# Shorter register heads, narrower frame copies, and variances ahead of the last sums in small units

## The reference, cut to what matters

```python
def _gn(v, G=32, eps=1e-5):
    g = v.reshape(B_, G, C_ // G, H_, W_)
    m = jnp.mean(g, axis=(2, 3, 4), keepdims=True)
    s = jnp.var(g, axis=(2, 3, 4), keepdims=True)
    return ((g - m) / jnp.sqrt(s + eps)).reshape(v.shape)
# in _displace: offset -> off_int (rounded) and sub (rest); kern = exp(-(kx*kx+ky*ky)/(2*0.5**2)), normalised
shifted = x[:, ch[:, None, None], iyc[:, :, None], ixc[:, None, :]] * mask[None]
out = lax.conv_general_dilated(shifted, kern_c[:, None, :, :], window_strides=(1, 1), padding='SAME', ...)
x = x + _displace(_gn(x), offset)
```

## Time and profile before

| | us |
|---|---|
| median of three runs | 976.3 |
| the profiled execution's own time | 979.06 |
| its span on the core | 977.1 |
| TensorE busy, mean granted clock 0.888 | 785.6 |
| VectorE busy | 824.8 |
| ScalarE busy | 638.9 |
| GpSimd busy | 368.1 |
| data moved | 403.09 MB, 413 GB/s |

### The profile page before, as it was taken

How to read it: one execution, slowest core, us unless ns; L and a number is a source line. 1 busy time by engine, 2 the same in 40 slices (tenths; PEclk the granted TensorE clock), 3 DMA queues, 4 the chain that set the end, 5 groups by cost and what they waited for, 6 DMA issues and landing times.

```text
span 977.1 us, 9088 instructions
## 1 busy us (share of the span) xinstructions
PE 785.6 (80%) x2132; PEld 383.6 (39%) x2132; DVE 824.8 (84%) x551; ACT 638.9 (65%) x461; POOL 368.1 (38%) x348
## 2 busy tenths in 40 slices
PE   0998987979979698897979879689797997979820
PEld 0544443434434343353434434345343443434410
DVE  7587988777798997978889899898998979797795
ACT  7778676564766747678466746577675785774661
POOL 0214034340432624013254393463845438250312
PEclk9999988989979799897998979989898897989955
DMA  9999999999999999999999999999999999999948
GB/s 364 427 401 423 392 405 429 429 429 428 430 429 430 432 428 414 430 429 430 431 429 406 398 433 376 407 419 393 431 408 430 430 427 431 431 431 430 430 208 343
DMA packets 27821, 403.09 MB, mean 413 GB/s; under 512 B 3216, under 2 KB 3216, under 8 KB 3216
## 3 DMA queue, kind: packets, MB, share of 16 engines
q1 hardware_dynamic: 27792, 402.71, 98.0%
HBM read 201.38 MB, written 201.33 MB: 412 GB/s over the span
## 4 chain that ended last, share of the span: by engine, by line
DVE 28%; DMA 27%; PE 20%; POOL 7%; issue 7%; ACT 5%; DVEq 3%; ACTq 2%; SPq 0%; POOLq 0%
PE sum_ps L289 17%; DMA out_dram<-xs 15%; DMA xs<-x_dram 12%; DVE xs L713 6%; DVE xs L716 6%; DVE smooth L709 6%; DVE smooth L704 6%; DVE xs L719 4%; POOL small L253 2%; POOL small L260 2%; ACT frame L417 2%; POOL small L257 2%; ACT unused L484 2%; POOL small L266 1%; ACTq L393 1%
## 5 line engine op out<-in xcount | busy, mean ns | idle before, releaser
L289 PE MATMUL sum_ps<-xs,bands 128*128 128x512 f32 x976 | 483.5, 653 | 51.2 <-DMA xs<-x_dram 51.2
L484 ACT ACTIVATE unused<-xs,small 128x4096 bf16 (+1 forms) x94 | 348.3, 3706 | 8.3 <-ACT small L470 4.8
L417 ACT ACTIVATE frame<-xs,small (+1 forms) x96 | 223.3, 2326 | 184.3 <-DVE smooth L709 183.3
L289 PEld LDWEIGHTS sum_ps<-xs,bands 128*128 128x128 f32 x976 | 200.6, 210 | 295.4 <-issue 282.2
L253 POOL TENSOR_TENSOR small<-small 128x3 f32<-128x3 f32 x32 | 41.6, 1299 | 570.6 <-ACT small L492 570.6
L289 PE MATMUL sum_ps<-xs,halves 128*128 128x512 f32 x496 | 230.0, 619 | 17.4 <-DMA xs<-x_dram 17.4
L704 DVE SCALAR_TENSOR_TENSOR smooth<-frame,side_w 128x612 f32 (+5 forms) x96 | 163.6, 1705 | 72.2 <-ACT frame L417 37.1
L713 DVE SCALAR_TENSOR_TENSOR xs<-smooth,small,xs 128x612 f32 (+5 forms) x96 | 163.5, 1703 | 51.9 <-POOL small L266 49.6
L709 DVE SCALAR_TENSOR_TENSOR smooth<-frame,side_w,smooth x96 | 159.7, 1664 | 7.5 <-DVE smooth L704 4.1
L719 DVE SCALAR_TENSOR_TENSOR xs<-smooth,small,xs 128x594 f32 (+9 forms) x96 | 159.8, 1664 | 3.4
L716 DVE SCALAR_TENSOR_TENSOR xs<-smooth,small,xs 128x594 f32 (+9 forms) x96 | 159.7, 1664 | 3.4
(11 more groups left out here) (132 smaller groups left out, 259.3 us busy)
## 6 DMA issues: line engine op xcount, KB each, us to landing
xs<-x_dram SPq DMA_DIRECT2D x96, 2048.0 KB, 14.8
out_dram<-xs SPq DMA_DIRECT2D x96, 2048.0 KB, 17.7
smooth<-offset_dram SPq DMA_DIRECT2D x1, 48.0 KB, 4.1
```

The source lines that it names most:

```text
L289: last = nc.tensor.matmul(sum_ps[:, :], (FIRST, SAME, SECOND)[i], slot_px(n, c * BANK, (c + 1) * BANK), start=(i == 0 and c == 0), stop=(i ...
L417: nc.scalar.activation(frame[:, bass.ds(b, rows * PITCH)].rearrange("p (r c) -> p r c", c=PITCH)[:, :, LEFT:LEFT + W], xs[:, bass.ds(a, ro ...
L484: nc.scalar.activation(unused[:, :], xs[:, bass.ds(n % SLOTS * PIX, PIX)], ACT.Square, bias=neg_mean[:, i:i + 1], accum_out=squares[:, i:i ...
```

## The change

Four things are changed.

1. **VectorE's head.** The table has a fifth number for each tile (`BESIDE`), so that the head no longer computes the address of the neighbour column. What L709's address needs (`turn`, `behind`) is computed after L704 has been issued. The loop counts from 1, and `side_w` has one more column for it.
2. **ScalarE's copy.** Where the window has 34 columns or fewer, the copy takes 34 columns instead of 64, and 64 or 34 rows: `COPIES` has six sizes (four of 64 columns, then 64x34 and 34x34) instead of four. The table for it is computed by more steps on VectorE at the start.
3. **TensorE's order** in small units: the variances of u stand before the sums of u+1's third tile, as in large ones.
4. **ScalarE's order** in small units: `variances(u)` stands before `sum_means(u + 1)`.

```diff
-    WORDS = 4
-    KIND, TO, FROM, COLUMN = range(WORDS)
+    WORDS = 5
+    KIND, TO, FROM, BESIDE, COLUMN = range(WORDS)
+    NARROW = 2
+    COPIES = [(rows, W) for rows in SIDES] + [(SIDES[k], SIDES[NARROW]) for k in (0, NARROW)]
+    COL_BITS = (W - SIDES[NARROW]).bit_length()
...
-                    early = UT if u % 2 else UT - 1
-                    sums(u + 1, range(early))
+                    sums(u + 1, range(UT - 1))
                     variances(u)
-                    sums(u + 1, range(early, UT))
+                    sums(u + 1, range(UT - 1, UT))
                     means(u + 1)
...
-                row = word & (1 << ROW_BITS) - 1
-                rows_kind = act.snap(word >> ROW_BITS)
+                column = word & (1 << COL_BITS) - 1
+                row = (word >> COL_BITS) & (1 << ROW_BITS) - 1
+                copy_kind = act.snap(word >> ROW_BITS + COL_BITS)
...
-                    rows = SIDES[k]
+                    rows, cols = COPIES[k]
...
-                        frame[:, bass.ds(b, rows * PITCH)].rearrange("p (r c) -> p r c", c=PITCH)[:, :, LEFT:LEFT + W],
-                        xs[:, bass.ds(a, rows * W)].rearrange("p (r c) -> p r c", c=W),
+                        frame[:, bass.ds(b, rows * PITCH)].rearrange("p (r c) -> p r c", c=PITCH)[:, :, LEFT:LEFT + cols],
+                        xs[:, bass.ds(a, rows * W)].rearrange("p (r c) -> p r c", c=W)[:, :, 0:cols],
...
+                variances(u, first)
                 if ahead and not large:
-
                     sum_means(u + 1)
-                variances(u, first)
...
-            chained(V.scalar_tensor_tensor(code[:, :, 0], kind[:, :, 1], float(1 << ROW_BITS), first_row[:, :, 1],
+            chained(V.tensor_scalar(narrow, kind[:, :, 0], float(NARROW), None, ALU.is_ge))
+            chained(V.tensor_scalar(low, kind[:, :, 1], float(NARROW), float(len(SIDES)), ALU.is_ge, ALU.add))
...
+            chained(V.scalar_tensor_tensor(code[:, :, 0], code[:, :, 0], float(1 << COL_BITS), narrow,
                                            ALU.mult, ALU.add))
...
+                turn = kind_of % 2
+                behind = (src + 1 - turn).with_bounds(min_val=1, max_val=most + 1)
...
-                dve.reg_mov(at_turn, kind_of & 1)
-                turn = dve.snap(at_turn, min_val=0, max_val=1)
-                dve.reg_mov(at_behind, src + 1 - turn)
-                dve.reg_mov(at_beside, src + 2 * turn - 1)
-                beside = dve.snap(at_beside, min_val=0, max_val=FRAME_ROWS * PITCH)
+                beside = dve.snap(next_tile[BESIDE], min_val=0, max_val=FRAME_ROWS * PITCH)
```

More of the change, by code:

```diff
@@ L104, in build @@
         base_w = xs[:, SLOTS * PIX:].rearrange("p (n k) -> p n k", k=3)
-        side_w = [sb(f"side_w{k}", [P, TILES]) for k in range(2)]
+        side_w = [sb(f"side_w{k}", [P, TILES + 1]) for k in range(2)]
         words = sb("words", [P, WORDS * (TILES + 1)], i32)
-        fills = sb("fills", [P, TILES], i32)
+        fills = words[HALF:P, 0:TILES]
         setup = smooth[:, 0:11 * 2 * POSITIONS].rearrange("p (n f a) -> p n f a", n=11, a=2)
@@ L404, in fill_frame @@
                 act.reg_mov(frames, u * UT + i)
-                act.reg_mov(copy_from, base + row * W)
-                act.reg_mov(copy_to, row * PITCH + PAD * PITCH)
+                act.reg_mov(copy_from, base + row * W + column)
+                act.reg_mov(copy_to, row * PITCH + column + PAD * PITCH)
+                source = act.snap(copy_from, min_val=0, max_val=SLOTS * PIX)
+                target = act.snap(copy_to, min_val=PAD * PITCH, max_val=FRAME_ROWS * PITCH)
+                done = act.snap(frames, min_val=1, max_val=TILES)
                 if i == 0:
@@ L596, in for_halves @@
                 return column.rearrange("p (j t) -> p j t", t=2 * UT).unsqueeze(2).to_broadcast(
-                    [P, len(PAIRS), HALVES, 2 * UT])
+                    [column.shape[0], len(PAIRS), HALVES, 2 * UT])
             FAR, ROUNDER = 1024.0, 1.5 * 2.0 ** 23
@@ L680, in _, with smooth_tile @@
             V.engine_nop().then_inc(tile_done, 1)
-            next_tile = [dve.alloc_register(name) for name in ("next_kind", "next_to", "next_from", "next_column")]
+            next_tile = [dve.alloc_register(name) for name in
+                         ("next_kind", "next_to", "next_from", "next_beside", "next_column")]
             done_count = dve.alloc_register("done_count")
-            at_turn, at_beside, at_behind = (dve.alloc_register(name) for name in ("turn", "beside", "behind"))
-            def smooth_tile(rows, cols, src, beside, behind, turn, dst, n, done, weights):
+            def smooth_tile(rows, cols, src, beside, kind_of, most, dst, done, weights):
                 under = xs[:, bass.ds(dst, rows * W)]
@@ L700, in smooth_tile @@
                 sm = smooth[:, 0:rows * cols].rearrange("p (r c) -> p r c", c=cols)
-                part = smooth[:, bass.ds(turn, rows * cols)].rearrange("p (r c) -> p r c", c=cols)[:, :, 0:cols - 1]
                 dve.wait_ge(frame_ready, done)
-                V.scalar_tensor_tensor(sm, frame_window(beside, cols), side_w[0][:, bass.ds(n, 1)], frame_window(src, cols),
+                V.scalar_tensor_tensor(sm, frame_window(beside, cols), side_w[0][:, bass.ds(done, 1)], frame_window(src, cols),
                                        ALU.mult, ALU.add
@@ L708, in smooth_tile @@
                 dve.reg_load(next_tile, words[0:1, bass.ds(done * WORDS, WORDS)])
-                V.scalar_tensor_tensor(part, frame_window(behind, cols - 1), side_w[1][:, bass.ds(n, 1)], part,
+                turn = kind_of % 2
+                behind = (src + 1 - turn).with_bounds(min_val=1, max_val=most + 1)
+                part = smooth[:, bass.ds(turn.with_bounds(min_val=0, max_val=1), rows * cols)].rearrange(
+                    "p (r c) -> p r c", c=cols)[:, :, 0:cols - 1]
+                V.scalar_tensor_tensor(part, frame_window(behind, cols - 1), side_w[1][:, bass.ds(done, 1)], part,
                                        ALU.mult, ALU.add
@@ L741, in emit @@
                     smooth_tile(rows, cols, src.with_bounds(min_val=1, max_val=most),
-                                beside.with_bounds(min_val=0, max_val=most + 1),
-                                behind.with_bounds(min_val=1, max_val=most + 1), turn,
+                                beside.with_bounds(min_val=0, max_val=most + 1), kind_of, most,
                                 dst.with_bounds(min_val=0, max_val=(SLOTS - 1) * PIX + (H - rows) * W + W - cols),
-                                n, done, weights)
+                                done, weights)
                 choose(dve, kind_of, 0, len(SIDES) ** 2, emit, 2)
@@ L750, in _ @@
             dve.addr_align(256, max_nops=0)
-            with dve.Fori(0, TILES) as n:
+            with dve.Fori(1, TILES + 1) as n:
                 tile_of(n)
```

50 lines of the change are left out of this document (31 added, 19 removed).

## The result

| | before | after |
|---|---|---|
| median of the runs, us | 976.15 (4 runs, 973.61 to 976.35) | 1017.42 (4 runs, 1012.62 to 1024.46) |
| profiled execution, its own time, us | 979.06 | 1012.62 |
| ratio of the medians | | 1.0435, 95% interval 1.0371 to 1.0498 |

The forecast was 971.9, in a range that ended at 976.5. It was wrong by 45.5 us and in sign. The mechanism that did it was not among the rivals.

The account below looks back on a forecast made before the run. Transfers were taken to bound most of the kernel, VectorE 501 to 747 us and the end. Units 16 to 23 -5.2, new order +0.9, start +0.7, end -0.8 made -4.4: 976.3 to 971.9 us, range 967.5 to 976.5.

Parts of the forecast that it names:

- VectorE's head: Units 16 to 23: 13 exposed heads 0.5 us shorter, 1.0 lost behind the table read, net -5.5 us of VectorE's time.
- The stretch of units 16 to 23, -5.2: 501 to 747 us, VectorE-bound: units 16 to 19 keep 3.4 us, units 20 to 23 can give 1.8.
- if the next part eats it: Low end, -1 us, of the gain in units 16 to 23, should the part after them take it.
- The end, -0.8: From tile 90 on: exposed heads save 1.2 us, L709's longer waits in the last two tiles cost 0.4.
- That the offset is carried over: Whole kernel: the profiled execution's 2.8 us above the median kept, the terms' -4.4 applied to 976.3 us.
- The weights, -2.1: Small units, 501 to 747 us: variances leave earlier, taking 2.1 of L713's 4.2 us wait for weights.
- The new order, +0.9: Small units: the second copy comes 1 to 2.8 us later, costing 0.1 in each of four units, 0.5 later.
- the second copy hands the gain back: Rival, chance 0.20: later sums delay small units' second copy, taking the 3.4 us of units 16 to 19; 975.3 us.
- slower rival: Rival, chance 0.08: in small units TensorE waits for squares before the variances, and its clock may drop; +4.0, 980.3 us.
- the weights come no earlier: Rival, chance 0.10: GpSimd's steps beside VectorE keep L713's 2.1 us wait; +1.0 in units 16 to 19, 972.9 us.
- The start, +0.7: Setup: fourteen more instructions make the first store 1.4 us later; small units 1 and 3 give some back.
- The narrow copies: ScalarE's copies: time goes by elements, 0.86 to 1.6 us shorter each, buying slack only; nothing counted of its own.

Follow-up runs that it names:

- r5s5: The kernel before with the changed kernel's whole table (rows of five words, 20 bytes apart, ScalarE's word in the same tensor): 1027.28 us, ratio 1.0529.
- aligned4: The changed kernel with table rows of four words at multiples of 16 bytes, the weights' column worked out in registers behind L738: 974.36 us, ratio 0.9984.
- r4off8: The kernel before with its table moved by 8 bytes, the read still four words: 1009.26 us, ratio 1.036.
- heads_only: The kernel before with the shorter heads alone, on aligned rows of four words, old order, full-width copies: 974.03 us, ratio 0.998.
- aligned4_order: aligned4 with the old order in small units on both TensorE and ScalarE: 972.46 us, ratio 0.9969.
- narrow_only: The kernel before with the narrower copies and their fourteen setup instructions alone, old heads, old order: 977.44 us, ratio 1.0016.
- after_head4: The changed kernel with VectorE's loop as before and four words a row; narrower copies and new order stay: 976.09 us, ratio 1.0001.
- r4x1: The kernel before with its aligned read of four words split into four reads of one word: 1079.96 us, ratio 1.1064.

## Why the prediction was wrong

**The step that failed** stands under "VectorE's head": against the heads "one more register row stands behind the table read and in front of L709", "0.1 to 0.2 us each, 1.0 in all". I took the read to take as long after the change as before, and let the fifth word cost nothing. It went from a median of 590 to one of 1894 ns. r5s5 puts 51 us on that table in the kernel before, and the changed kernel against aligned4 gives 43 (1017.4 less 974.4). I had priced the row behind the read (0.25 + 0.05 in after, where one row of 0.09 stood before, about what I had said) and not the read.

Two things led there. I inferred the read from the few tiles in which L709 waited, and did not look at the line of L708, whose 340/590/1336 shows that it varies fourfold. That it is short only because it is one step came out of r4off8. And the nearest row was misleading too: ScalarE's read of one word takes as long as VectorE's of four,

```profile
L393 ACTq TENSOR_LOAD <-fills x96: 274/590/1179, 22.2 to 955.2; - x96
```

so a price without regard to the number of words looked right. It isn't: four words are one step only on a multiple of 16 bytes. The Trainium skill's page "Runtime: NRT & Kernel Launch", section "Instruction fetch mechanics", puts a register load at about 200 ns for each register, even in bulk. The page speaks of the loads that the runtime adds, from HBM. Before's 340 ns for four words from SBUF does not agree with it, but the steps of 0.2 to 0.24 off the grid do. By that figure the fifth word would have been, as an estimate, 0.2 us in every head where the read is exposed.

No rival of mine let the read itself get longer, and one should have.

**The other terms**, judged with the read mended:

- *The stretch of units 16 to 23, -5.2.* Tiles 48 to 72 took 239.9 us in aligned4 (498.04 to 737.89) against 245.6: -5.8, right in the trace. The mechanism was right too: the waits for L704 that no data ends fell from 11.6 to 4.5 us in 501 to 747 us, in aligned4 and in heads_only, where these tiles took 4.3 us less than before, and the wait of the instruction behind the read rose by 1.2 in aligned4 (0.7 to 1.9), where I had said 1.0. GB/s there rose from 410 to 420, as forecast:

```profile
501.00:747.00 246.00, 209.01 (x557) 99.61 (x555) 229.06 (x123) 149.25 (x113) 144.08 (x85) 0.92 1.00 420
```

- *That this stays to the end.* At tile 72 aligned4 was 8.8 us ahead of before (737.89 and 746.66), 5.8 of it from this stretch. At tile 90 it was 3.7 ahead (914.20 and 917.85): tiles 72 to 90 took 176.3 us, where before took 171.2, both at 430 GB/s. So 5.1 of the 5.8 went again. 176.3 is 36 transfers of 4.90 us; before, I take it, had been behind its transfers and could catch up. That is the end of my range that I had called "if the next part eats it", and I gave it too little.
- *The end, -0.8.* From tile 90 to the end of the span aligned4 took 57.4 us and before 59.3: -1.9. (The three heads of my working, 0.5, 0.5 and 0.3, add up to 1.3 and not to 1.2.)
- *That the offset is carried over.* I added all terms to one execution that lay 2.8 us above the median. Between the profiled executions aligned4 gains 5.4 us (979.06 to 973.62), between the medians 1.4. The executions of before lie between 973.3 and 979.6, so part of what its trace showed as lost was that execution's own and not there to be won. At tile 48 aligned4 is 3.0 us ahead of it (498.04 and 501.03), for which I had no term. This is argued from the differences, not shown: every kernel has one trace.
- *The weights, -2.1.* Right in size: L742's wait for them in 501 to 747 us is 4.2 us in aligned4 and 6.7 in aligned4_order. But with the new heads VectorE comes sooner and waits as long as before (4.2). With the old heads the order takes off 0.7 there (2.6 in narrow_only, 1.9 in after_head4).
- *The new order, +0.9.* Its net effect was put at -1.2 (+0.9 - 2.1) and is +1.9 beside the new heads. It looks like the rival "the second copy hands the gain back", since the 60.1 us above stand where 17.6 did, but not where I had put it: in 501 to 747 us the wait for the copy is 3.1 us against 2.4. The time goes from tile 72 to tile 90, as shown above, and what costs it there stays open. Of the slower rival's other half little shows: TensorE's wait for squares ahead of the variances (L357) is 6.2 us over the span in aligned4 and 3.5 in aligned4_order, far from 2 us a unit. And the rival "the weights come no earlier" is wrong: their wait fell from 61.8 to 23.6.
- *The start, +0.7.* In after the first copy began at 29.96 us against 27.28 and took 2.14 for 2.99 us: it ended 1.8 later, where I had said 1.4. narrow_only makes it 1.4 for the whole kernel. In heads_only the first copy ends as before, yet L707 of tile 0 starts at 31.39 us against 30.48; what holds it 0.9 us I did not find out. In aligned4 the same instruction starts at 34.47 us, 1.9 behind the copy's end; it still waits for the weights afterwards (L742 for 4.2 us), so nothing is lost by that alone.
- *The narrow copies.* By elements, as chosen: 1.26 and 2.14 us for the two shapes. That they are worth 2 us beside the other parts I had not counted.

With all of this the change as I understood it would have been worth 1.4 us and not 4.4. The misses beside the read are 2.5 us (974.4 less 971.9); the read is 43.

## What to carry to other kernels

A register load from SBUF stands in an engine's queue like any instruction, so its length has to be read from the trace, with its spread, before its operand is changed. Keep table rows that are read in a loop at four words on a 16-byte grid, and get a fifth number by register arithmetic (0.2 us here, behind an instruction that hides it). If an instruction that is hidden gets longer, ask how much cover it has in the shortest iteration: here 0.55 us.

## What the runs showed of the hardware that was not expected

- The same four words cost 33 us more over 96 tiles when the table began 8 bytes later (median read 590 and 1617 ns).
- A one-word read takes 0.30 us with half the transfers and up to 1.3 with all of them (medians 304 and 426 ns; 145 of the 384 in r4x1 took over 0.8 us). The Trainium skill's page "DMA: Bandwidth & Descriptors", section "Latency and other measured facts", gives about 600 ns as the floor of a `tensor_load`, and does not say from where it loads. The shortest here took 297 ns, from SBUF.
- With slow reads the time varies more: 1012.6 to 1024.5 us in four runs of the changed kernel and 1075.8 to 1093.5 in four of r4x1, against 973.3 to 979.6 in 29 runs of the kernel before.
